# One semaphore for each third of a batch's gathered rows, in a fused four-part transformer kernel

## The reference

```python
x = x + einsum('bct,bcd->bdt', x, weights[conditions])        # L0: one 64x64 matrix per batch
# L1: attention over a paged cache
q, k, v = x @ Wq, x @ Wk, x @ Wv                              # then norm and rotation of q and k
k_blocks = k_blocks.at[blk, :, off, :].set(k)                 # new rows go into the shared pool
v_blocks = v_blocks.at[blk, :, off, :].set(v)
k_all, v_all = k_blocks[block_tables], v_blocks[block_tables] # pages of each batch
p = softmax(where(window of 256 keys, q @ k_all, -inf))
x = x + (p @ v_all) @ Wo
x = x + x @ W[id] + b[id]                                     # L2: one 512x512 expert per batch
x = x + x @ W3 + scaled low-rank adapter of the batch         # L3
```

## Time and profile before

| what | value |
| --- | --- |
| median of 3 runs | 1107.1 us (1106.96 to 1110.6) |
| profiled execution, span | 1135.0 us (no time around the span is given for it) |
| PE busy | 1048.5 us, 92% of the span |
| PEld (weight loads) busy | 709.2 us, 62% |
| DVE busy | 660.7 us, 58% |
| ACT busy | 539.0 us, 47% |
| POOL busy | 535.0 us, 47% |
| mean granted TensorE clock | 0.968 of full |
| DMA moved | 196.16 MB, mean 173 GB/s |

### The profile page before, as it was taken

The page is one execution under the profiler, slowest core; times in us unless marked ns, Lnnn a source line. Parts: engine busy times, 40 slices in busy tenths (PEclk is TensorE's granted clock), DMA queues, the critical chain, the costliest instruction groups (busy, mean ns, idle before and its releaser), DMA issues.

```text
span 1135.0 us, 23836 instructions
## 1 busy us (share of the span) xinstructions
PE 1048.5 (92%) x6438; PEld 709.2 (62%) x6438; DVE 660.7 (58%) x1928; ACT 539.0 (47%) x1337; POOL 535.0 (47%) x597
## 2 busy tenths in 40 slices
PE   7989999997588999999999999999899998999998
PEld 6767777675355566666556666666565666666665
DVE  5889896667344555555555555555455454555552
ACT  4457776674344444434444444444344444444441
POOL 3555444366555454554454545454354454454400
PEclk9999999999579999999999999999899899999999
DMA  3434443563367666565666666666565565566641
GB/s 130 143 116 149 140 146 115 176 197 119 95 205 208 191 194 200 185 195 168 209 201 187 189 202 187 183 207 207 157 202 187 174 203 189 172 185 181 220 141 59
DMA packets 95337, 196.16 MB, mean 173 GB/s; under 512 B 31346, under 2 KB 40114, under 8 KB 87110
## 3 DMA queue, kind: packets, MB, share of 16 engines
q1 hardware_dynamic: 63942, 149.49, 41.0%
q0 software_dynamic: 30784, 44.16, 14.0%
q10 hardware_dynamic: 576, 2.10, 0.5%
HBM read 195.08 MB, written 33.56 MB: 201 GB/s over the span
## 4 chain that ended last, share of the span: by engine, by line
PE 64%; issue 3%; ACT 3%; another core or an unknown queue 2%; DMA 1%; POOL 1%; DVE 0%; ACTq 0%; POOLq 0%; DVEq 0%
PE bank L93 22%; PE bank L1476 11%; PE bank L1451 9%; PE bank L1430 8%; PE bank L1438 8%; PE bank L1417 4%; ACT PT L1230 2%; PE bank L1407 1%; ACT KT L1230 1%; DMA KV<-kv_scratch,idxs 1%; DMA KV<-in_pool,idxs 1%; POOL KV L1132 0%; POOL KVE L1142 0%; POOL KV L1142 0%
## 5 line engine op out<-in xcount | busy, mean ns | idle before, releaser
L1230 ACT ACTIVATE PT<-bank 112x384 f32<-112x384 f32 x256 | 113.7, 489 | 271.7 <-PE bank L1438 225.3
L1308 DVE CUSTOM_DVE_ANT_0 SM<-bank,FM 128x336 f32<-128x336 f32 x256 | 129.7, 507 | 162.2 <-PE bank L1430 121.4
L1142 POOL DMA_INDIRECT KV<-kv_scratch,idxs x96 | 96.1, 1001 | 128.1 <-DMA KV<-in_pool,idxs 104.9
L1142 POOL DMA_INDIRECT KVE<-kv_scratch,idxs_e x93 | 93.3, 1004 | 124.4 <-DMA KVE<-in_pool,idxs_e 99.9
L1239 ACT ACTIVATE PR<-SM,nb 128x336 f32<-128x336 f32 x256 | 145.5, 574 | 1.9 <-DVE nb L1312 1.7
L1132 POOL DMA_INDIRECT KV<-in_pool,idxs x96 | 95.4, 994 | 76.6 <-PE bank L1451 49.9
L1430 PE MATMUL bank<-KT,QB 64*128 64x336 f32 x512 | 113.2, 521 | 15.2 <-ACT KT L1230 11.6
L1132 POOL DMA_INDIRECT KVE<-in_pool,idxs_e x90 | 89.8, 998 | 73.7 <-PE bank L1451 46.9
L1230 ACT ACTIVATE KT<-bank 128x336 f32<-128x336 f32 x128 | 57.6, 450 | 140.0 <-PE bank L1417 132.5
L1476 PE MATMUL bank<-W,XT 128*64 128x512 f32 x512 | 123.7, 604 | 0.0
L1438 PEld LDWEIGHTS bank<-ident,PR 128*112 128x112 f32 x768 | 84.3, 137 | 48.9 <-issue 48.9
(11 more groups left out here) (195 smaller groups left out, 2167.6 us busy)
## 6 DMA issues: line engine op xcount, KB each, us to landing
W<-in_w SPq DMA_DIRECT2D x64, 1024.0 KB
FM<-mask SPq DMA_DIRECT2D x64, 168.0 KB
X<-in_x SPq DMA_DIRECT2D x32, 256.0 KB
x_scratch<-X SPq DMA_DIRECT2D x32, 256.0 KB
qt_scratch<-QT SPq DMA_DIRECT2D x32, 256.0 KB
QB<-qt_scratch SPq DMA_DIRECT2D x32, 256.0 KB
XB<-x_scratch SPq DMA_DIRECT2D x32, 256.0 KB
BB<-in_b SPq DMA_DIRECT2D x64, 128.0 KB
```

Of the source, the lines that this page charges most:

```text
L1142: pool.indirect_dma_start(out=KV[k][:, c, :], out_offset=None, in_=kv_d, in_offset=bass.IndirectOffsetOnAxis(ap=idxs[k][:, NCH + c:NCH + c ...
L1230: return nc.scalar.activation(dst, src, ACT.Copy)
L1308: v.tensor_tensor_reduce(out=SM[u % 2][:, :], in0=bank[u % 2][:, 0:SPAN], in1=FM[k][:, :], scale=1.0, scalar=-3e38, op0=ALU.add, op1=ALU.m ...
```

## The change

The semaphore `kv_old` of each of the four buffers becomes three, one for each third. Every gather of old rows signals the semaphore of its own third. `fresh(b)` no longer waits once for all three thirds; ahead of each gather of new rows it waits for the old rows of that third. The wait at L823 is cut up in the same way. `landed(b)` on SP now waits for the three semaphores one after the other. There are 8 more semaphores; no transfer is added or removed, and no DMA changes its place in a queue.

```diff
-        s_old_e = [sem(f"kv_old{i}") for i in range(2)]
+        s_old_e = [[sem(f"kv_old{i}_{c}") for c in range(NCH)] for i in range(2)]
...
-                            bounds_check=NPOOL * BLOCK - 1, oob_is_err=False).then_inc(s_old_e[b], 16)
+                            bounds_check=NPOOL * BLOCK - 1, oob_is_err=False).then_inc(s_old_e[b][c], 16)
...
                 pool.wait_ge(s_kvo, 16 * PAIRS)
-                pool.wait_ge(s_old_e[0], 16 * NCH)
                 for c in range(NCH):
+                    pool.wait_ge(s_old_e[0][c], 16)
                     pool.indirect_dma_start(
...
-            s_old = s_old_e + [sem(f"kv_old{i}") for i in range(2, 4)]
+            s_old = s_old_e + [[sem(f"kv_old{i}_{c}") for c in range(NCH)] for i in range(2, 4)]
...
-                                bounds_check=NPOOL * BLOCK - 1, oob_is_err=False).then_inc(s_old[k], 16)
+                                bounds_check=NPOOL * BLOCK - 1, oob_is_err=False).then_inc(s_old[k][c], 16)
...
-                        wait_all(pool, s_pass_pool, (s_old[k], at(pr.i, 16 * NCH, 16 * NCH - 1)))
                         for c in range(NCH):
+                            wait_all(pool, s_pass_pool, (s_old[k][c], at(pr.i, 16, 15)))
                             pool.indirect_dma_start(
...
-                            wait(sp, s_old[2 * ahead.par + 1 - b], at(ahead.i, 16 * NCH, 16 * NCH - 1))
+                            for c in range(NCH):
+                                wait(sp, s_old[2 * ahead.par + 1 - b][c], at(ahead.i, 16, 15))
```

## The result

The changed kernel took 1100.32 us (median of 5 runs, 1097.51 to 1101.85) against 1106.96 us (5 runs, 1105.18 to 1110.6) for the kernel before beside it: ratio 0.9937 [0.9921, 0.9953]. It is 6.6 us faster; 2.0 us were forecast. The kernel before takes 1105.6 to 1107.7 us in the median on two chips, as in this comparison, and 1126.7 and 1127.9 us on two others; I call them the 1107 us and the 1127 us kind. Each of the slower two was used on one occasion only, so whether it is the chip or the occasion isn't shown.

A forecast was written before the change was run, and what follows sets the result against it. TensorE, busy 92% of the span, was taken to set the end, with gathers holding it up only in the opening. Terms 1.4 + 0.6 + 0 = 2.0 us less than 1107.1 gave 1105.1 us, range 1100.0 to 1110.6.

The forecast's parts named there:

- Settled pairs, worth 0: Settled pairs: new rows issued up to 2.6 us earlier on POOL, where they already had 10.1 us of room; worth 0.
- Extra semaphores, worth 0: SP's expert loads and already met waits on POOL: more semaphores cost 0, by the row at 304.93; upper end 0.3 us each.
- POOL's gain of 2.5 us at the first batch: Opening of the second part, pair 1: POOL's new gathers of batch 0 end at 302.1 instead of 304.62, 2.5 us earlier.
- 1.4 us at pair 1's scores: TensorE's wait for queries (QB) before pair 1's scores: QB comes at 317.2 instead of 318.64, a gain of 1.4 us.
- sharing: Pair 2's earlier gathers of old rows share the DMA engines with QB, which takes back 1.1 us.
- The cap of 2.2 us by ScalarE's copy of keys: Pair 1's scores can't start ahead of ScalarE's last copy of keys at 316.4, so at most 2.2 us come out.
- 0.6 us in the second place: TensorE's 0.61 us wait at 322.21 for new rows of batch 1 goes whole: 0.6 us.
- Nothing is late next, because the value products behind it (322.93) had no idle time: Behind the wait at 322.21 in pair 1: nothing further holds TensorE up, so the 0.6 us counts in full.
- All hidden: Rival, opening: thirds land bunched, or sharing eats the 2.5 us; no gain, 1107.1 us; chance 0.22.
- A sooner clock: Rival, pair 1: with TensorE's gap gone its full clock returns sooner, 3.6 us more, 5.6 in all, 1101.5 us; chance 0.17.
- Collision: Rival: pair 2's earlier gathers hold QB back, TensorE's clock stays low past 328; 6.5 us slower, 1113.6 us; chance 0.11.
- The range: Whole kernel: from 1100.0 us (clock case with its best end) to 1110.6 us (forecast's worst end and 2 us between runs).

The follow-up runs named there:

- h2: Changed kernel, but thirds waited for apart only from pair 4 on, all three up front in pairs 0 to 3; 1107 us kind: 1.0013 of the kernel before.
- e3: Changed kernel, but thirds waited for apart only from pair 4 on, all three up front in pairs 0 to 3; 1127 us kind: 1.0256 of before.
- f1: The changed kernel again, unedited, on a chip of the 1127 us kind: 1.018 of the kernel before.
- e1: Changed kernel with its 12 semaphores, but POOL waits for all three thirds ahead of the first new gather; 1127 us kind: 1.0026 of before.
- h0_before: The kernel before, unchanged, profiled again on a chip of the 1107 us kind: 1.0001 of before, span 1107.3 us.
- h1: Changed kernel, but thirds waited for apart only in pairs 0 to 3, all three up front from pair 4; 1107 us kind: 0.9955 of before.

## Why the prediction was wrong

The direction, the change's place and its first link were right; the size, 2.0 us against 6.6, was 3.3 times too small.

*Settled pairs, worth 0*: right within 0.25% on the 1107 us kind (`h2` 1.0013 [1.0001, 1.0025]). POOL's idle time changed lines as said. On the 1127 us kind the same part costs about 2% (`e3` 1.0256, `f1` 1.018), which no row that I had would have shown.

*Extra semaphores, worth 0*: right as far as can be measured (`e1`, `h2`). But I misread the row for it: at 304.93 POOL waits for one semaphore, `gather_args3`, as the listing under The change shows, and not for two.

*POOL's gain of 2.5 us at the first batch*: right. From first scores to the first expert load it takes 19.5 us in `h0_before` and 17.0 after.

*1.4 us at pair 1's scores*: near. Measured 1.1, or 1.8 in the mean of five profiles; from QB's issue to its use 7.9 us in `h0_before`, 9.3 after, so sharing took 1.4 where I had 1.1. The cap of 2.2 us by ScalarE's copy of keys was no cap: in the profile that I read, TensorE had waited 2.54 us for a copy of keys at 308.69 and ran at the low level from there (its scores took 1.49 us), so it came late; in `h0_before` it waited 8.51 us for QB there. That error did not decide, since the gain was limited by the sharing.

*0.6 us in the second place*: the wait of 0.61 us for new rows is not in `h0_before`, so nothing was there to gain; it does stand in `h2`, and is gone in `h1`.

*"Nothing is late next, because the value products behind it (322.93) had no idle time"*: this step failed, and the sum with it. I stopped the chain at pair 1 and put everything behind it at nothing. POOL's chain of gathers does not end there: before, a batch takes 10.5 us of it, or 13.6 beside an expert load, 24.1 a pair, hardly less than TensorE's 24.4. Such a chain gains hardly any lead, and as long as it has none TensorE can have to wait for it again, in `h0_before` at pair 2. With the thirds apart a batch takes 8.0 to 8.4 us, or 12.5 to 12.9 beside a load, waits for TensorE taken out: about 21 a pair, some 3 us less than TensorE needs. SP's second load, the queries and the new rows of pair 2 hang on that chain. What it was worth: 5.5 of the 6.6 us, in the second and third pair, against `h0_before`, 3.5 in the mean of the five profiles, where I had 0; of the 5.1 us of the third pair there, 3.15 are clock. The 0.3 us by which 24.1 is below 24.4 could have been worked out beforehand: in the profile that I had, POOL's first wait for TensorE comes only at 390 us, and I read it to 315.37.

```profile
390.35 0.99 POOL L1132 DMA_INDIRECT KV<-in_pool,idxs  x1 [2.54 <-PE bank L1451]
```

The waits that the chain makes could not be read off there: that profile has neither the 8.51 us for QB nor the 2.36 us at pair 2. How the gain splits between waiting and clock in other executions isn't measured.

*The rivals*. All hidden: refuted by the ratio. A sooner clock: at the wait for QB the granted clock falls within the wait and stays low for 10.3 us in both kernels (317.0 to 327.3, 315.0 to 325.3), so not where I put it; a later low stretch of 7 us, 351.1 to 358.0, is what went. Collision: sharing was seen, at 1.4 us, and the clock penalty behind it was not. The page "TensorE: Matmul & The Clock Gate" of the Trainium skill, section "What's actually happening", has activity release the throttle; the trace agrees in that both low stretches of `h0_before` come with a wait of TensorE (the first begins inside the one of 8.51 us, the second just behind the one of 2.36) and end while TensorE works without a gap.

*The range*: its lower end should have been 1107.1 - 3.6 - 2.8 = 1100.7, not 1100.0. The measured 1100.3 lies between the two, and it came about in another way than that rival's.

The thirds in the opening only are the version to keep where it isn't known which chip will run it: 0.9955 (`h1`) on one kind, 1.001 [0.9972, 1.0047] (`e2`) on the other. It is not faster than the changed kernel on the first kind (0.9937), so nothing beats both kernels everywhere.

## What to carry to other kernels

Where a helper engine's own chain of issue and wait is nearly as long as the period of the engine that sets the time (24.1 against 24.4 us here), a cut at each link adds up until the helper has slack: follow that chain to its first wait for the bound engine before the sum is closed. A wait that vanishes on reordering a queue is not yet gained; sum several periods, since it may stand one period later. And a gain below 1% in waits between engines has to be timed on more than one chip.

## What was not expected of the hardware

- The same program takes 1105.6 to 1107.7 us on two chips (and 1107.0 in the first comparison) and 1126.7 and 1127.9 us on two others, and a change can be 0.6% faster on the one kind and 1.8% [1.4, 2.2] slower on the other. Each of the slower chips was used once.
- On the slower kind, TensorE's completion signals are recorded late, in the changed kernel's settled pairs up to 2.3 us after the matmul's end; the place in the pair was another with the loop's thirds apart (12 us in) than with them together (4 and 22 us in).
- Waits on POOL for rows that have landed cost nothing beyond the 0.30 us between two issues; one for rows still on their way shows as 0.4 to 1.5 us in the changed kernel's settled pairs and up to 5.1 us in the opening.
- Gathering the old rows of each pair's second batch 5 to 7 us later made the kernel 7.0% slower (`g3`).
